# Narrow self-attentions of a decoder: 32-row score products over a bf16 mask, Newton inverse roots on tile pairs, ten unused products in early tiles

## What is computed

```python
def rmsnorm(x, w): return x * rsqrt(mean(x * x) + 1e-6) * w
def qk_norm(x):    return x * rsqrt(mean(x * x) + 1e-6)      # over the 8 values of a head
# attention with 16 query heads, 4 key/value heads, 8 values each
q, k = rope(x @ wq), rope(x @ wk)                            # global: k, v through a latent of 32
q, k = qk_norm(q), qk_norm(k)
scores = where(mask, q @ k.T / sqrt(8), -1e30)               # causal; local: also distance < 32
out = softmax(scores) @ v @ wo
h = layernorm(x)
h = h + global_attention(rmsnorm(h, norm1_w))
h = h + local_attention(rmsnorm(h, norm2_w))
x = x + h
```

## Time and profile before

| | us |
|---|---|
| median of three runs | 2465.9 |
| the profiled execution's own time | 2468.1 |
| its span | 2466.3 |
| TensorE busy | 2193.3 (89% of the span) |
| VectorE busy | 1922.4 (78%) |
| ScalarE busy | 1516.2 (61%) |
| GpSimd busy | 1225.4 (50%) |
| global stage, setup to last addition | 1081.2 to 1399.5 |
| local stage, setup to last addition | 1400.5 to 1704.1 |

### The profile page before, as it was taken

How to read it: one execution, slowest core, us unless ns; L and a number is a source line. 1 busy time by engine, 2 the same in 40 slices (tenths; PEclk the granted TensorE clock), 3 DMA queues, 4 the chain that set the end, 5 groups by cost and what they waited for, 6 DMA issues and landing times. The chain is left out here.

```text
span 2466.3 us, 90321 instructions
## 1 busy us (share of the span) xinstructions
PE 2193.3 (89%) x33103; PEld 1800.5 (73%) x33103; DVE 1922.4 (78%) x5481; ACT 1516.2 (61%) x4037; POOL 1225.4 (50%) x1215
## 2 busy tenths in 40 slices
PE   7999999978777753439999799998999999999998
PEld 7888888865555531228888588886888888888886
DVE  3888888868999986988888667775777777777786
ACT  1666666657777776538888588885444444444443
POOL 0333333327777752029999699994232232232232
PEclk9999999999999986659999899999999999999999
DMA  5000000000000000010000000000000000000000
GB/s 122 3 0 0 0 0 0 0 5 21 18 19 18 18 8 1 1 34 2 0 0 0 1 2 0 0 0 5 9 14 12 13 11 11 13 11 11 13 11 14
DMA packets 56944, 25.67 MB, mean 10 GB/s; under 512 B 18115, under 2 KB 56326, under 8 KB 56838
## 3 DMA queue, kind: packets, MB, share of 16 engines
q1 hardware_dynamic: 53426, 23.06, 3.5%
q10 hardware_dynamic: 3412, 1.19, 0.2%
HBM read 20.04 MB, written 4.19 MB: 10 GB/s over the span
## 5 line engine op out<-in xcount | busy, mean ns | idle before, releaser
L706 POOL TENSOR_TENSOR sa_sc<-sa_sc,sa_rs 128x1024 f32<-128x1024 f32 x64 | 121.9, 1904 | 314.1 <-DVE sa_rs L682 314.1
L1856 POOL TENSOR_TENSOR lo_qk_r<-lo_qk_ms,w_neg_half 128x20 f32<-128x20 f32 x64 | 227.0, 3546 | 21.8 <-DVE lo_qk_ms L1779 21.8
L1856 POOL TENSOR_TENSOR gl_qk_r<-gl_qk_ms,w_neg_half 128x20 f32<-128x20 f32 x64 | 226.9, 3545 | 1.5 <-DVE gl_qk_ms L1779 1.4
L486 POOL TENSOR_TENSOR xan_ve<-xan_mv,w_eps_ln 128x1 f32<-128x1 f32 x64 | 12.1, 190 | 398.2 <-DVE xan_mv L480 398.2
L892 ACT ACTIVATE xa_cT<-xa_misc 128x128 f32<-128x128 f32 x64 | 17.8, 277 | 302.9 <-PE xa_misc L793 273.6
L1016 POOL TENSOR_TENSOR xa_sc<-xa_sc,xa_rs 128x1024 f32<-128x1024 f32 x64 | 121.7, 1901 | 120.1 <-DVE xa_rs L976 120.1
L821 PEld LDWEIGHTS xa_qs<-xan_xT,late_x_wq 128*128 128x128 f32 x1024 | 119.1, 191 | 52.2 <-issue 52.2
L973 DVE TENSOR_REDUCE xa_sm<-xa_sc 128x16 f32<-128x1024 f32 x64 | 78.1, 1220 | 72.7 <-ACT xa_sc L916 72.7
L558 PE MATMUL sa_qs<-san_xT,w_a_wq 128*128 128x128 f32 x1024 | 130.0, 280 | 2.7 <-DVE sa_sc L668 2.2
L821 PE MATMUL xa_qs<-xan_xT,late_x_wq 128*128 128x128 f32 x1024 | 131.3, 281 | 0.0
L832 PE MATMUL xa_pp<-xa_cT,late_x_wk 128*128 128x128 f32 x1024 | 131.1, 281 | 0.0
(11 more groups left out here) (332 smaller groups left out, 6918.5 us busy)
## 6 DMA issues: line engine op xcount, KB each, us to landing
w_x<-in_x_dram SPq DMA_DIRECT2D x8, 512.0 KB, 7.5
ca_cx<-in_ctx_dram SPq DMA_DIRECT2D x64, 64.0 KB, 1.8
xa_cx<-in_ctx_dram SPq DMA_DIRECT2D x64, 64.0 KB, 1.7
out_dram<-xa_out SPq DMA_DIRECT2D x64, 64.0 KB, 1.6
ca_mask<-in_mask_BxSxS_ff_dram SPq DMA_DIRECT2D x64, 32.0 KB, 1.7
w_a_wq<-in_L_attn_Wq_dram SPq DMA_DIRECT2D x1, 512.0 KB
w_a_wo<-in_L_attn_Wout_dram SPq DMA_DIRECT2D x1, 512.0 KB
prep_xwo<-in_L_xattn_Wo_dram ACTq DMA_DIRECT2D x1, 512.0 KB
```

The lines of the kernel that those rows point to most:

```text
L706: pool.tensor_tensor(v, v, bcast(rs[:, s, :], 2, S), ALU.mult).then_inc(prob_done, 1)
L1856: pool.tensor_tensor(qk_r[:, s, :], qk_ms[:, s, :], k["neg_half"][:, 0:NQK], ALU.pow).then_inc(sg["qk_r"], 1)
```

## The change

In words, with the new lags:

- **Scores.** The queries are turned as one 128x128 tile and so are the keys, which VectorE has written four times over (`kn`, now 128 columns). ScalarE copies both at once (`queries_keysT`). GpSimd writes the keys' four masked copies (`key_blocks`, first in its list, lag 6). The mask is now added by four bf16 products of a unit matrix with the mask (256 columns each), and the scores by 16 products on tiles of 32 rows (K is 32, 128 by 64 columns), accumulated onto it. Each part of 32 rows writes a bank of its own.
- **Roots.** The 20 inverse roots of a tile become 40 of a pair: VectorE halves and seeds by integer arithmetic on the bits, for odd tiles only (`qk_halve`, `qk_seed`, last in its list), and GpSimd does three Newton steps of four operations each, every operation waiting for the one before (`qk_rsqrt`, last in its list, lag 2).
- **Norms.** In the global stage the root-mean-square norm's factor is computed from the layer norm's variance: one power of two columns, and `rms_measure`, `rms_mean`, `rms_square`, `rms_epsilon`, `rms_apply` fall away there.
- **Unused products.** For t an integer, `turn` first multiplies the unit matrix by itself ten times into an unused part of the bank. `start` becomes 16, so these are the tiles 0 to 14, and tile 63, whose turn is in the steps after the loop.
- **Order.** The lags grow: turning of queries and keys 6, scores 6, attend 7, output 8; TensorE's and ScalarE's loops hold eight steps. Setup: the clearing of `qT` and `kz` and eight copies fall away, two copies to bf16 come.

```diff
-        rot, sq = sb("rot", [P, 2, NQK, HD]), sb("sq", [P, 2, NQK, HD])
+        rot, sq = sb("rot", [P, 4, NQK, HD]), sb("sq", [P, 2, NQK, HD])
...
-        kn = sb("kn", [P, 2, KVG, HD])
+        kn = sb("kn", [P, 2, 4, KVG, HD])
...
+        identb, maskb = sb("identb", [P, P], BF16), sb("maskb", [P, 4, S], BF16)
...
                     after(pe, sg["normed"], t)
                     after(pe, sg["hT"], t, 1)
-                    pe.transpose(misc[:, 0:P], hn[:, s, :], ident).then_inc(sg["hT_psum"], 1)
+                    after(pe, sg["qT"], t, 6)
+                    for n in range(10 if isinstance(t, int) else 0):
+                        pe.matmul(tr[:, 3 * P:4 * P], ident, ident, start=True, stop=True)
+                    pe.transpose(tr[:, 0:P], hn[:, s, :], ident).then_inc(sg["hT_psum"], 1)
...
+                    pe.wait_ge(sg["hT"], min(t + 5, NT) if isinstance(t, int) else t + 5)
+                    pe.transpose(tr[:, P:2 * P], qn[:, s, :, :, :].rearrange("p r g d -> p (r g d)"), ident)
+                    pe.transpose(tr[:, 2 * P:3 * P], kn[:, s, :, :, :].rearrange("p r g d -> p (r g d)"), ident).then_inc(sg["qkT_psum"], 1)
+
+                def scores(t, four):
+                    s = four % 2
+                    after(pe, sg["exp"], t, 1, per=2)
                     for r in range(4):
+                        pe.matmul(ss[:, r, 0:256], identb[:, :], maskb[:, :, :].rearrange("p n i -> p (n i)"), start=True, stop=False)
                     after(pe, sg["qT"], t)
+                    after(pe, sg["k_blocks"], t)
+                    gate(k, pe)
                     for b in range(2):
                         for g in range(2):
+                            for r in range(4):
+                                q = slice(r * 32, r * 32 + 32)
+                                last = pe.matmul(ss[:, r, (2 * b + g) * 64:(2 * b + g) * 64 + 64],
+                                                 kz[q, s, b, 2 * g:2 * g + 2, :].rearrange("p g j -> p (g j)"),
+                                                 qkT[q, s, 0, b * 64:b * 64 + 64], start=False, stop=(b == 1 and g == 1))
+                    last.then_inc(sg["scores_psum"], 1)
...
-                skewed(pe, NT, [(4, turn_queries_keys), (6, turn_out), (2, project), (5, attend), (6, output), (1, turn), (4, scores)], 4)
+                skewed(pe, NT, [(6, turn_queries_keys), (1, turn), (2, project), (7, attend), (8, turn_out), (6, scores), (8, output)], 8)
...
+                def queries_keysT(t, four):
+                    s = four % 2
                     after(act, sg["qkT_psum"], t)
+                    act.wait_ge(sg["hT_psum"], min(t + 6, NT) if isinstance(t, int) else t + 6)
+                    after(act, sg["scores_psum"], t, 2)
+                    after(act, sg["k_blocks"], t, 2)
+                    act.activation(qkT[:, s, :, :].rearrange("p n i -> p (n i)"), tr[:, P:3 * P], ACT.Copy).then_inc(sg["qT"], 1)
...
-                skewed(act, NT, [(4, queriesT), (6, outT), (4, key_blocks), (2, values), (1, turned), (4, exponent)], 4)
+                skewed(act, NT, [(6, queries_keysT), (1, turned), (8, outT), (2, values), (6, exponent)], 8)
...
+                def qk_halve(t, four):
+                    if four % 2:
+                        p = slice(four - 1, four + 1)
+                        after(dve, sg["qk_ms"], t)
+                        after(dve, sg["qk_r"], t, 4)
+                        dve.tensor_scalar(qk_half[:, p, :], qk_ms[:, p, :], HD * EPS_RMS, 0.5, ALU.add, ALU.mult).then_inc(sg["qk_half"], 2)
+
+                def qk_seed(t, four):
+                    if four % 2:
+                        p = slice(four - 1, four + 1)
+                        after(dve, sg["qk_half"], t)
+                        after(dve, sg["qkn"], t, 4, per=2)
+                        dve.tensor_scalar(qk_r[:, p, :].bitcast(I32), qk_half[:, p, :].bitcast(I32), -0.5, SEED, ALU.mult,
+                                          ALU.add).then_inc(sg["qk_seed"], 2)
...
+                    skewed(dve, NT, [(6, qk_apply), (1, rms_apply), (9, residual), (0, rms_measure), (9, residual_x), (0, rms_mean),
                                      (2, rotate), (0, rms_square), (2, rotate_sum), (0, rms_epsilon), (2, qk_measure),
+                                     (7, invert_sums), (2, qk_sum), (7, divide), (2, qk_halve), (2, qk_seed)], 4)
                 else:
...
+                    skewed(dve, NT, [(6, qk_apply), (1, normed_hidden), (9, residual), (0, hidden), (1, hidden_itself),
+                                     (0, hidden_mean), (2, rotate), (0, hidden_epsilon), (2, rotate_sum), (2, qk_measure),
+                                     (7, invert_sums), (2, qk_sum), (7, divide), (2, qk_halve), (2, qk_seed)], 4)
...
+                    for n in range(3):
+                        if n == 0:
+                            after(pool, sg["qk_seed"], t)
+                        else:
+                            pool.wait_ge(sg["qk_step"], t - 1 + n)
+                        done = (t - 1) * 3 + 2 * n + 2
+                        pool.tensor_tensor(y2, y, y, ALU.mult).then_inc(sg["qk_y2"], 2)
+                        pool.wait_ge(sg["qk_y2"], done)
+                        pool.tensor_tensor(y2, y2, qk_half[:, p, :], ALU.mult).then_inc(sg["qk_hy2"], 2)
+                        pool.wait_ge(sg["qk_hy2"], done)
+                        pool.tensor_tensor(y2, three_halves[:, :, :], y2, ALU.subtract).then_inc(sg["qk_rest"], 2)
+                        pool.wait_ge(sg["qk_rest"], done)
+                        last = pool.tensor_tensor(y, y, y2, ALU.mult)
...
+                def key_blocks(t, four):
+                    s = four % 2
+                    after(pool, sg["qT"], t)
+                    after(pool, sg["scores_psum"], t, 2)
+                    pool.tensor_tensor(kz[:, s, :, :, :].rearrange("p b g j -> p g b j"),
+                                       bcast(qkT[:, s, 1, :].rearrange("p (b j) -> p b j", b=2), 1, KVG),
+                                       bcast(bcast(groups, 2, 2), 3, S), ALU.mult).then_inc(sg["k_blocks"], 1)
...
+                skewed(pool, NT, [(6, key_blocks), (0, rms_rsqrt if local else rsqrt), (2, qk_rsqrt)], 4)
```

More of the change, by code:

```diff
@@ L8 @@
 BF16 = mybir.dt.bfloat16
+I32 = mybir.dt.int32
 ALU = mybir.AluOpType
@@ L29 @@
 DROPPED = -1.0e30
+SEED = float(0x5f3759df - 0x400000)
 CONSTS = {}
@@ L1614, in attend @@
-                def attend(t, four):
-                    s = four % 2
+                            for r in range(4):
+                                q = slice(r * 32, r * 32 + 32)
+                                last = pe.matmul(ss[:, r, (2 * b + g) * 64:(2 * b + g) * 64 + 64],
+                                                 kz[q, s, b, 2 * g:2 * g + 2, :].rearrange("p g j -> p (g j)"),
+                                                 qkT[q, s, 0, b * 64:b * 64 + 64], start=False, stop=(b == 1 and g == 1))
@@ L1616, in attend @@
+                    last.then_inc(sg["scores_psum"], 1)
+                def attend(t, eight):
+                    s = eight % 2
                     after(pe, sg["exp"], t, per=2)
@@ L1620, in attend @@
                         for b in range(2):
[L1621 to L1622 removed]
+                            last = pe.matmul(av[b * 64:b * 64 + 64, n * 2 * VW:(n + 1) * 2 * VW], pr[:, s, n % 4, b, n // 4, :],
+                                             vz[:, eight, n // 4, b, :, :].rearrange("p e d -> p (e d)"), start=True, stop=True)
                     last.then_inc(sg["av_psum"], 1)
@@ L1675, in exponent @@
                     after(act, sg["av_psum"], t, 2)
-                    for b in range(2):
-                        act.wait_ge(sg["scores_psum"], t * 2 + b + 1)
-                        act.activation(pr[:, s, :, b, :], ss[b][:, :].rearrange("p (n i) -> p n i", i=S), ACT.Exp,
+                    after(act, sg["scores_psum"], t)
+                    for r in (0, 2):
+                        act.activation(pr[:, s, r:r + 2, :, :, :].rearrange("p r b g i -> p r (b g i)"), ss[:, r:r + 2, 0:256], ACT.Exp,
                                        scale=HD * float(HD) ** -0.5).then_inc(sg["exp"], 1)
@@ L1715, in rms_measure @@
                     s = four % 2
-                    if not local:
-                        after(dve, sg["hidden"], t)
-                        gate(k, dve)
                     dve.bn_stats(rstats[:, s, :], tile_of(H, t)).then_inc(sg["rms_stats"], 1)
@@ L1852, in qk_rsqrt @@
                 def qk_rsqrt(t, four):
-                    s = four % 2
-                    after(pool, sg["qk_mse"], t)
-                    after(pool, sg["qkn"], t, 2, per=2)
-                    pool.tensor_tensor(qk_r[:, s, :], qk_ms[:, s, :], k["neg_half"][:, 0:NQK], ALU.pow).then_inc(sg["qk_r"], 1)
-                shift = 0 if local else 2
-                front = [] if local else [(0, rsqrt)]
-                skewed(pool, NT, front + [(shift, rms_rsqrt), (2 + shift, qk_rsqrt)], 4)
```

(10 more changed lines are left out.)

112 lines of the change are left out of this document (44 added, 68 removed).

## The result

The kernel after takes 2829.72 us (median of three, 2824.38 to 2831.18) against 2465.9: ratio 1.1456, 95% interval 1.144 to 1.1472. The forecast was 2575, its range 2475 to 2670. Slower was right; of the 364 us lost the forecast had 109. The profiled execution took 2829.72, its span is 2827.7.

The account below looks back on a forecast made before the run. TensorE's list (4.4 us) and GpSimd's powers were taken to bound the 4.48 us global step neck and neck, TensorE the local one. Global +51, local +61, setup -3, together +109, gave 2575; range 2475 to 2670.

Parts of the forecast that it names:

- rival 2: Loops of both stages: TensorE, less busy, is granted half clock, list 7.1, total 2775 (2625 at mean 0.8); chance 0.08.
- fifty steps of 5.1: Global loop after the unused products, to the last pair's scores: 5.1 us per step, from 1175 to 1430.
- The stage summed: Global stage from first turn to last addition: 357.9 us, ending at 1450.2 against 1399.5, +51.
- Way to the first attend: Start of the global stage: first turn at 1092.3, first attend at 1119.
- TensorE's list at full clock: TensorE's own work per step: 3.57 us, with masks 0.6, scores 0.7 and attend 1.05.
- The ring of attend and exponent: Per step, attend through turn, masks, scores and two exponents to the next attend: 3.86 us, the best step.
- The burst: GpSimd's Newton work: twelve dependent 128x40 operations at 0.35 us each, 4.2 us per pair of tiles.
- the ring over two steps: Attend, reciprocal, seed, Newton work, key blocks, scores, exponents, attend two steps on: 9.75 us, 10.15 with the seed late.
- the mechanism that led the forecast: Key blocks queue behind GpSimd's Newton work, so every second tile's come 2.0 us late and TensorE stands at scores.
- Rival 1: Loops of both stages: key blocks not late, step 3.86 from step 16 on, total 2453; chance 0.15.
- Rival 4: Scores on TensorE: 32-row products stand in line, 4.1 us instead of 0.7, pair 13.5, total 2740; chance 0.04.
- rival 3: VectorE and GpSimd exclude each other throughout, seed 0.7 late, pair 12.05, step 6.0, total 2665; chance 0.11.

Follow-up runs that it names:

- experiment 2: Kernel after without any unused products; 2805.94 us, ratio 1.135 to the kernel before.
- experiment 3: Kernel after with one Newton step instead of three; 2752.05 us, ratio 1.1132 to the kernel before.
- experiment 9: Kernel after with one Newton step and one unused product in every tile; 2507.53 us, loosely known, ratio 1.0154 to the kernel before.
- experiment 5: Kernel after with its roots undone: one GpSimd power of 20 columns per tile, no seed, no Newton steps; 2818.71 us, ratio 1.1409 to the kernel before.
- 6: Kernel after with score products reading all 128 rows instead of 32, so not computing the layer; 3240.05 us, ratio 1.3114 to the kernel before.
- 1: Kernel after with the ten unused products in every tile, also in the hardware loop; 2836.59 us, ratio 1.1474 to the kernel before.
- experiment 7: Kernel after with mask and unit matrix in f32 instead of bf16; 2706.16 us, ratio 1.0953 to the kernel before.
- 8: Kernel after with one Newton step and three unused products in every tile; 2547.38 us, ratio 1.0311 to the kernel before.
- 10: Kernel after with three Newton steps kept and three unused products in every tile; 2750.51 us, ratio 1.1137 to the kernel before.

## Why the prediction was wrong, step by step

**The step that failed is rival 2, with its 0.08.** The text says "Against: the list stays dense in bursts of 3 us", and takes full clock for all of the loop: the term of the sum that failed is its fifty steps of 5.1, which were 7.01 at a granted 0.50. Its working was right: "at the half level in the loop the list is 7.1" (7.01 measured) and 2775 (2829.72). What was wrong was to take TensorE's busy time as the sign of its clock. 99% busy at 1.00 in the earlier trace rows was read as the cause of 1.00; the loops of the kernel after and of experiments 2 and 3 are busy for all of the time at 0.50, and that of experiment 9 for 95% of it at 1.00.

**The stage summed.** From first turn to last addition the global stage took 485.7 (1090.7 to 1576.4; before 303.9), the forecast 357.9; the local one 483.5. The 127.8 too few:
- Loop: 46 steps, 7.01 instead of 5.1: 88.
- Way to the first attend: 43.7 instead of 26.7 (1134.39 against 1119): 17. In the first turns the products ran mostly at the half level, 3.7 to 4.6 us for twenty records where the sum had 2.56 from the second tile on, and instead of lying in TensorE's idle time they came behind each late norm. The first of them:

```profile
1090.72 4.61 PE L1589 MATMUL gl_tr<-w_constant 128*128 128x128 f32 x20 [13.66 <-DVE gl_hn L1717]
```

- The first ten steps: 68.6 instead of 60.9: 8, from late key blocks of up to 2.9 and the fall. The products themselves took 2.23 to 2.32 at full clock (to the turn behind them), under the forecast's 2.56.
- Last seven steps and drain: 45.0 and 5.8 instead of 31.9 and 3.6: 15, the half level again (the last four were to take 3.9; at full clock two took 4.12, at half 6.34).

**TensorE's list at full clock**, 3.57 forecast, was 3.88: turns 0.22 and 0.11, projection 0.43, attend 1.05, turn 0.17, masks 0.53 (0.6 forecast), output 0.32 as forecast or less; scores 1.05 instead of 0.7. I had taken the 0.69 of sixteen longer records for the thirty-two short ones; they start 0.033 apart, and their 1.05 lies between that row's total and the upper bound of 4.1. The ring of attend and exponent, 3.86, becomes 4.12, as the steps without burst show.

**The burst**, 4.2 forecast, was 4.8: twelve operations 0.40 apart (forecast 0.35), most of them 0.25 to 0.27 long. With TensorE at half clock:

```profile
1304.23 0.25 POOL L1876 TENSOR_TENSOR gl_qk_a<-gl_qk_r 128x40 f32<-128x40 f32 x1 [1.36 <-DVE gl_qk_r L1793]
1304.63 0.29 POOL L1878 TENSOR_TENSOR gl_qk_a<-gl_qk_a,gl_qk_half 128x40 f32<-128x40 f32 x1
...
1308.62 0.27 POOL L1882 TENSOR_TENSOR gl_qk_r<-gl_qk_r,gl_qk_a 128x40 f32<-128x40 f32 x1
1309.03 1.21 POOL L1892 TENSOR_TENSOR gl_kz<-gl_qkT,w_constant 128x512 f32<-128x512 f32 x1
```

Only the length of one was right; its completion and the next start cost 0.14, not 0.08. With 4.8 and scores of 1.05 the ring over two steps is 5.55 + 0.35 + 4.8 + 0.4 (the seed's delay, as forecast) = 11.1, step 5.55. The trace of the kernel after has it at full clock only where the level then falls: from the attend to the late scores 9.43 (1189.60 to 1199.03) and 8.93 (1539.37 to 1548.30), where this sum has 8.65. With scores, exponents and the way to the next attend at full clock (1.05 + 1.4) that makes a pair of 11.4 to 11.9, a step of 5.7 to 5.95, as an estimate. So the mechanism that led the forecast was right and undersized: at full clock it would have cost 0.5 to 0.9 a step more than forecast. It is not what the kernel after pays for in its loop, and no run shows the kernel after's own list at a held full clock.

**The other rivals.** Rival 1 (no late key blocks) is false at full clock and, in the loop as it ran, true in an odd way: they are hidden by a slower TensorE. Even its premise gives no gain: with one Newton step and a held clock the step is 4.5. (Its 2453 is worked out from the profiled time of 2577, the other rivals' from the median; from 2575 it is 2451.) Rival 4 is out: 1.05, not 4.1. Of rival 3, the part on the seed was right: VectorE's operations on two tiles in SBUF stretch beside the key blocks. VectorE at the time of the key blocks above:

```profile
1309.01 0.32 DVE L1769 TENSOR_TENSOR gl_rot<-gl_rc,gl_rsn 128x160 f32<-128x160 f32 x1
1309.37 1.05 DVE L1774 TENSOR_TENSOR gl_sq<-gl_rot 128x160 f32<-128x160 f32 x1
```

1.05 instead of 0.33: it started inside the key blocks (1309.03 to 1310.24) and ended behind them. The trace agrees with what the prediction cites from the Trainium skill, "SBUF — State Buffer", "Who interferes with whom", on instructions with two SBUF inputs. Beside the burst itself the stretching stays small: of the twelve operations from 1192.54 on, four take 0.10 to 0.17 longer.

**Setup and start.** Minus 3 forecast between the stages; 4.5 instead of 7.7, so right. The norm's power of two columns: 0.75 forecast, 0.69 to 0.78 measured, median 0.77.

**What is left open.** Why this list is granted half the clock. Not the Newton roots (experiment 5), not late key blocks alone (3), not the 32 rows alone (6, though all 128 rows held the level longer); f32 products of full height and 128 or 256 columns, added to the same list, bring it up (1, 7, 8, 9), with three Newton steps and three products only in part (10). Whether it is the short scores, the bf16 masks or the old scores' absence as a whole was not separated further: experiment 7 changes the masks' type and doubles their records at once.

## What to carry to other kernels

When a change replaces the products that fill TensorE, forecast its clock as a term of its own with a large chance: read the granted clock of a stretch with the same kind of products, and don't infer it from busy time, which here rose to 100% because the clock was low. Before adding unused products, try one in every tile against ten in a few. And when a change has parts, time the one that relieves the engine at its limit alone: here it was worth 0.4%, and the rest cost 15%.

## What the runs showed of the hardware

- TensorE busy 260 of 260 us at a granted clock of 0.50 (experiment 3; 370 of 370 in experiment 2); one more product of 0.42 us per step of 7.0, and it went to 1.00 (9 against 3).
- Work that is more but of another kind can be faster: f32 masks, +1.3 us of products per step at full clock, 124 us less in all (7).
- A level can swing without settling: 1.00 for 10 to 21 us, 0.50 for 3 to 14, through both loops (10).
- GpSimd: dependent operations of 128x40 start 0.40 apart though each is 0.25 to 0.27 long.
